# Masked attention on one core: the context division on GpSimd, moments split over VectorE and ScalarE, inverse sums from repeated columns

## The reference

```
q = heads(x @ Wq + bq);  k = heads(x @ Wk + bk);  v = heads(x @ Wv + bv)
scores = einsum('bhqd,bhkd->bhqk', q, k) / sqrt(64)
probs  = softmax(scores + where(adj, 0, -9e15), axis=-1)
ctx    = einsum('bhqk,bhkd->bhqd', probs, v)
y      = x + ctx @ Wf + bf
out    = (y - mean(y)) / sqrt(var(y) + 1e-5)
```

## Time and profile before

| what | value |
|---|---|
| time of three runs | median 1284.17 us (1280.67 to 1289.34) |
| the profiled execution: its time | 1280.71 us |
| the profiled execution: its span | 1278.9 us |
| busy PE / DVE / ACT / POOL | 1177.3 / 1057.7 / 737.2 / 655.1 us |
| DMA moved, mean rate | 251.66 MB, 197 GB/s |
| mean granted clock of TensorE | 0.986 |

### The profile page before, as it was taken

One profiled execution on the slowest core, in us unless ns is written; L12 is line 12 of the kernel. 1 busy time (PEld: TensorE's weight loads), 2 busy tenths in 40 slices (PEclk: granted clock), 3 DMA queues, 4 the chain that ended last, 5 costly groups with the idle time before them and its releaser, 6 DMA issues.

```text
span 1278.9 us, 23768 instructions
## 1 busy us (share of the span) xinstructions
PE 1177.3 (92%) x8406; PEld 867.3 (68%) x8406; DVE 1057.7 (83%) x1619; ACT 737.2 (58%) x1404; POOL 655.1 (51%) x956
## 2 busy tenths in 40 slices
PE   6998999999999899989999899998999999998874
PEld 5866777666776677666776667766677666776642
DVE  5788887988789887889869889698887988789882
ACT  4665665656556575566655565555664656555540
POOL 1335662646536565474545665355762656535533
PEclk9999999999999999999999999999999999999997
DMA  5678877897778877888877978779877897868883
GB/s 163 148 192 234 190 198 192 201 237 175 201 191 215 228 189 195 198 222 201 205 186 188 237 186 211 181 188 248 190 195 186 205 242 176 206 165 204 211 195 96
DMA packets 111607, 251.66 MB, mean 197 GB/s; under 512 B 27904, under 2 KB 62336, under 8 KB 111488
## 3 DMA queue, kind: packets, MB, share of 16 engines
q1 hardware_dynamic: 111488, 250.13, 78.9%
HBM read 36.11 MB, written 12.58 MB: 38 GB/s over the span
## 4 chain that ended last, share of the span: by engine, by line
PE 53%; SPq 16%; DVE 16%; ACT 5%; issue 4%; DMA 3%; POOL 2%; DVEq 0%; POOLq 0%
PE context_ps L515 17%; SPq L307 15%; PE score_ps L500 13%; PE job_ps L406 7%; DVE prob L683 7%; PE job_ps L408 6%; PE job_ps L407 6%; ACT prob L606 5%; DVE prob L676 5%; DMA prob_t<-prob 3%; PE job_ps L437 2%; DVE res L700 1%; DVE stats L707 1%; POOL xt_lo L793 1%; SPq L370 1%
## 5 line engine op out<-in xcount | busy, mean ns | idle before, releaser
L606 ACT ACTIVATE prob<-prob,row_min 128x1024 f32<-128x1024 f32 x384 | 440.9, 1149 | 252.8 <-DVE row_min L676 252.8
L676 DVE CUSTOM_DVE_ANT_0 prob<-score_ps,mask 128x1024 f32<-128x1024 f32 x384 | 454.7, 1221 | 144.8 <-PE score_ps L500 122.7
L683 DVE STREAM_TRANSPOSE prob<-prob 128x1024 f32<-128x1024 f32 x384 | 458.9, 1233 | 31.7 <-ACT prob L606 31.7
L515 PE MATMUL context_ps<-prob_t,v_all 128*64 128x256 f32 x3072 | 359.8, 388 | 40.0 <-DMA prob_t<-prob 39.8
L515 PEld LDWEIGHTS context_ps<-prob_t,v_all 128*64 128x64 f32 x3072 | 236.0, 140 | 151.3 <-issue 58.6
L775 POOL TENSOR_SCALAR mask<-adj_in 128x1024 f32<-128x1024 uint8 x64 | 68.1, 1064 | 169.6 <-DVE row_min L676 156.2
L500 PE MATMUL score_ps<-k_hi,q_hi 64*128 64x512 f32 x768 | 140.7, 444 | 10.5 <-DVE row_min L676 9.7
L809 POOL TENSOR_TENSOR context_lo<-context,context_hi 128x256 fp32r<-128x256 f32 x96 | 70.6, 735 | 142.0 <-ACT context_hi L613 142.0
L406 PE MATMUL job_ps<-xt_hi,weight_hi 128*128 128x256 f32 (+1 forms) x423 | 142.5, 337 | 0.6
L797 POOL TENSOR_TENSOR q_lo<-raw,q_hi 128x256 fp32r<-128x256 f32 x95 | 69.5, 734 | 139.1 <-ACT raw L598 139.1
L407 PE MATMUL job_ps<-xt_lo,weight_hi 128*128 128x256 f32 (+1 forms) x423 | 135.5, 320 | 0.0
(11 more groups left out here) (73 smaller groups left out, 1693.1 us busy)
## 6 DMA issues: line engine op xcount, KB each, us to landing
prob_t<-prob SPq DMA_DIRECT2D x1536, 128.0 KB, 2.4
res<-in_x_dram SPq DMA_DIRECT2D x32, 384.0 KB, 4.0
out_dram<-res SPq DMA_DIRECT2D x32, 384.0 KB, 3.0
x_in<-in_x_dram SPq DMA_DIRECT2D x30, 384.0 KB, 4.1
adj_in<-in_adj_dram SPq DMA_DIRECT2D x31, 256.0 KB, 2.9
res<-in_x_dram SPq DMA_DIRECT2D x1, 768.0 KB, 7.0
prob_t<-in_L_gnn_Wk_dram SPq DMA_DIRECT2D x1, 576.0 KB, 4.3
prob_t<-in_L_gnn_Wq_dram SPq DMA_DIRECT2D x1, 576.0 KB, 8.4
```

Of the source, the lines that this page charges most:

```text
L515: last = pe.matmul(context_ps[64 * head:64 * head + 64, 0:GQ], v_all[:, kt, col:col + HS], keys, start=(kt == 0), stop=(kt == TT - 1))
L606: nc.scalar.activation(probabilities(t), probabilities(t), ACT.Exp, scale=-1.0, bias=row_min[:, ring:ring + 1], accum_out=row_sum[:, s // ...
L676: nc.vector.tensor_tensor_reduce(probabilities(t), in_quarters(score_ps[:, head, :]), in_quarters(mask[:, s % 2, :]), 1.0, HUGE, ALU.add, ...
L683: nc.vector.transpose(probabilities(t), probabilities(t)).then_inc(squared, 1)
```

## The change

The change has eight parts.

1. `divide` moves from VectorE to GpSimd. Since GpSimd's division reads no PSUM, ScalarE first copies `context_ps` to a new tile `context_raw` (`take_context`, behind the slot's exponentials), and GpSimd multiplies `context_raw` by `context`. The next `mix` waits for the copy instead of the division.
2. `add_residual` becomes one `tensor_tensor_reduce`, which also adds up the row, and one small `tensor_scalar` that makes the negated mean. `moments` goes.
3. ScalarE gets `sum_squares`: a Square of the tile with the negated mean as bias, accumulated, at the start of the slot behind the one of the "p" job.
4. Variance plus epsilon and the first guess (`guess_root`) run on VectorE in slots 0, 8, 12, 18, between the masks and the transposes.
5. `make_diagonal` and the ones go. `spread_inverses` multiplies the inverse sums, one column repeated 64 times by an access pattern of step 0, by the identity: four matmuls of 128 columns in place of two of 256. It waits for the reciprocal.
6. GpSimd's order: the division ahead of low parts in its place of the table, `find_root` behind `context_low` in the same slot instead of at the slot's start. In the last slot VectorE refines the root.
7. Slot 9's order is q, x, p in place of q, p, x.
8. The two x loads of slots 11 and 12 (half 1) are issued by ScalarE behind its last eviction of x in slot 11; the last group's second 8 `move` DMAs are issued by ScalarE at slot 24 of the last batch.

```diff
-    9: [("q", 0, 2, 0), ("p", 0, 0, 0), ("x", 0, 0, 1)],
+    9: [("q", 0, 2, 0), ("x", 0, 0, 1), ("p", 0, 0, 0)],
-X_LOADS = {4: (0, 0), 6: (0, 1), 11: (1, 0), 12: (1, 1)}
+X_LOADS = {4: (0, 0), 6: (0, 1)}
+GUESSES = {0: -2, 8: -1, 12: 0, 18: 1}
...
             def spread_inverses(b, job):
-                pe.wait_ge(diag_done, at(b, GROUPS, job[1] + 3))
-                for head in range(2):
-                    last = pe.matmul(job_bank(b.mode, job)[64 * head:64 * head + 64, 0:GQ], ones[:],
-                                     diag[:, 2 * head:2 * head + 2, :], start=True, stop=True)
+                group = job[1]
+                pe.wait_ge(inverted, at(b, GROUPS, group + 1))
+                for qt in range(2):
+                    for head in range(2):
+                        col = 2 * head + qt
+                        last = pe.matmul(job_bank(b.mode, job)[64 * head:64 * head + 64, qt * P:(qt + 1) * P],
+                                         inv_sum[:, group % 2, col:col + 1].to_broadcast([P, HS]), ident[:],
+                                         start=True, stop=True)
...
             def mix(b, group):
-                pe.wait_ge(context_done, at(b, GROUPS, group + 2))
+                pe.wait_ge(context_out, at(b, GROUPS, group + 2))
...
+            def sum_squares(b, n):
+                group, tile = n // 2, n % 2
+                act.wait_ge(mean_done, at(b, TT, n + 1))
+                ...
+                nc.scalar.activation(squares[:], res[:, n % 4, :], ACT.Square, bias=mean_neg[:, n % 4:n % 4 + 1],
+                                     accum_out=square_sum[:, group % 2, tile:tile + 1]).then_inc(squares_summed, 1)
+            def take_context(b, group):
+                act.wait_ge(mixed, at(b, GROUPS, group + 3))
+                act.wait_ge(context_done, at(b, GROUPS, group + 2))
+                nc.scalar.activation(context_raw[:], context_ps[:, 0:GQ], ACT.Copy).then_inc(context_out, 1)
...
@@ ScalarE @@
             def body(b):
                 for s in slots_of(b.mode):
+                    if s > 0:
+                        for job in slot_work(b.mode, s - 1):
+                            if job[0] == "p":
+                                sum_squares(b, job[1])
+                    elif b.mode != "first":
+                        sum_squares(b, -3)
...
+                    if s == SLOTS:
+                        move(nc.scalar, b, GROUPS - 1, 1)
...
-                        if job[0] not in "pm" and job not in early:
+                        if job[0] == "m":
+                            take_context(b, job[1])
+                        elif job[0] != "p" and job not in early:
                             evict(b, job)
+                            if job == ("x", FT - 1, 0, 1):
+                                for i in range(2):
+                                    load_x(nc.scalar, b, 1, i)
...
@@ VectorE @@
             def add_residual(b, job):
-                nc.vector.tensor_tensor(res[:, n % 4, :], job_bank(b.mode, job)[:, 0:H], res[:, n % 4, :],
-                                        ALU.add).then_inc(sum_done, 1)
-            def moments(b, n):
-                ...
+                nc.vector.tensor_tensor_reduce(res[:, n % 4, :], job_bank(b.mode, job)[:, 0:H], res[:, n % 4, :],
+                                               1.0, 0.0, ALU.add, ALU.add,
+                                               row_total[:, n % 4:n % 4 + 1]).then_inc(sum_done, 1)
+                dve.wait_ge(sum_done, at(b, TT, n + 9))
+                nc.vector.tensor_scalar(mean_neg[:, n % 4:n % 4 + 1], row_total[:, n % 4:n % 4 + 1], -1.0 / H, None,
+                                        ALU.mult).then_inc(mean_done, 1)
+            def guess_root(b, group):
+                dve.wait_ge(squares_summed, at(b, TT, 2 * group + 2))
+                nc.vector.tensor_scalar(var_eps[:, two], square_sum[:, two], 1.0 / H, EPS,
+                                        ALU.mult, ALU.add).then_inc(var_done, 1)
+                ...
...
@@ GpSimd @@
+            def divide(b, group):
+                pool.wait_ge(context_out, at(b, GROUPS, group + 3))
+                pool.wait_ge(job_out, out_through(b, ("i", group, 0, 0)))
+                nc.gpsimd.tensor_tensor(context[:], context_raw[:], context[:], ALU.mult).then_inc(context_done, 1)
...
                     work = slot_work(b.mode, s)
                     for job in work:
+                        if job[0] == "m":
+                            divide(b, job[1])
                         if job[0] in "kqx":
                             low_part(b, job)
...
                     for group in contexts_split(b.mode, s):
                         context_low(b, group)
+                    if s in ROOTS and (ROOTS[s] >= 0 or b.mode != "first"):
+                        find_root(nc.gpsimd, b, ROOTS[s])
```

More of the change, by code:

```diff
@@ L300, in scale_rows @@
                 n = (2 * group + tile) % 4
-                engine.tensor_scalar(res[:, n, :], res[:, n, :], mean_var[:, group % 2, tile, 0:1],
+                engine.tensor_scalar(res[:, n, :], res[:, n, :], mean_neg[:, n:n + 1],
                                      inv_dev[:, group % 2, tile:tile + 1],
-                                     ALU.subtract, ALU.mult).then_inc(normalised, 1)
+                                     ALU.add, ALU.mult).then_inc(normalised, 1)
         def move_square(queue, group, a, c):
@@ L309, in move_square, with load_x, find_root, result @@
                             ).then_inc(landed[group % 2], 16)
+        def load_x(queue, b, half, i):
+            last_x = ("x", FT - 1, 1 - half, 1)
+            if half == 0 and b.mode == "first":
+                queue.wait_ge(job_done, 3)
+            else:
+                queue.wait_ge(job_done, done_through(b, last_x, 1 - half))
+            row = S + (4 * half + 2 * i) * P
+            queue.dma_start(x_in[:, 2 * i:2 * i + 2, :], x_rows[bass.ds(at(b, S, row), GQ), :].rearrange(
+                "(t p) h -> p t h", p=P)).then_inc(x_loaded[i], 16)
+        def find_root(engine, b, group):
+            engine.wait_ge(guess_done, at(b, 4, group + 1))
+            guess, var = inv_dev[:, group % 2], var_eps[:, group % 2]
+            ops = 0
+            def result(instruction):
+                nonlocal ops
+                ops += 1
+                instruction.then_inc(root_ops, 1)
+                engine.wait_ge(root_ops, at(b, 4 * ROOT_OPS, group * ROOT_OPS + ops))
+            for _ in range(NEWTON_STEPS):
+                result(engine.tensor_tensor(newton[:], guess, guess, ALU.mult))
+                result(engine.tensor_tensor(newton[:], newton[:], var, ALU.mult))
+                result(engine.tensor_scalar(newton[:], newton[:], -0.5, 1.5, ALU.mult, ALU.add))
+                result(engine.tensor_tensor(guess, guess, newton[:], ALU.mult))
+        def move(queue, b, group, part):
+            queue.wait_ge(squared, at(b, UNITS, 4 * group + 4))
+            queue.wait_ge(mixed, at(b, GROUPS, group + 1))
+            for ahead in (2 * part, 2 * part + 1):
+                for a in range(4):
+                    move_square(queue, group, a, (a + ahead) % 4)
         block = ctx.enter_context(nc.Block())
@@ L382, in body @@
                         load_residual(b, RES_LOADS[s])
[L383 to L384 removed]
+                    if s % 2 == 1 and (s < SLOTS - 1 or b.mode != "last"):
+                        move(sp, b, s // 2, 1)
                     if s % 6 == 1 and (s // 6 < 3 or b.mode != "last"):
@@ L725, in body @@
                         mask_scores(b, 2 * s + 1)
+                        if s in GUESSES and (GUESSES[s] >= 0 or b.mode != "first"):
+                            guess_root(b, GUESSES[s])
                         turn_squares(b, 2 * s)
                         turn_squares(b, 2 * s + 1)
-                    for job in work:
-                        if job[0] == "m":
-                            divide(b, job[1])
                     if s < SLOTS and s % 2 == 1:
```

112 lines of the change are left out of this document (30 added, 82 removed).

## The result

| | before | changed |
|---|---|---|
| median of 14 runs each, us | 1286.57 | 1291.9 |
| lowest to highest, us | 1280.67 to 1290.63 | 1289.97 to 1296.98 |
| profiled execution: its own time, us | 1280.71 | 1290.07 |
| its span, us | 1278.9 | 1288.3 |
| mean granted clock | 0.986 | 0.974 |

The ratio of the changed kernel to the one before is 1.0048, 95% interval 1.003 to 1.0066: half a per cent slower, where 1.25% faster was forecast. By the bound used in the prediction (1%) that is no change, but its sign is plain. The profiled execution of before was one of its fastest, so the two spans lie 9.4 us apart and the medians 5.3; for the size of an effect the ratios are used, and the traces for its place.

The account below looks back on a forecast made before the run. TensorE, busy 92%, was bounded by a chain of waits through slots 8 to 18. Seven batches gave 12.6 us, the last batch 1.2, the tail 2.2: 16 off 1284.2 gives 1268, range 1259 to 1277.

Parts of the forecast that it names:

- SyncE and DMA: Slots 11 to 14: two x loads moved to ScalarE land group 5's squares earlier, gaining 0 to 0.6 us, 0.4 taken.
- the split of the tail: Last group's 16 DMAs issued from two engines take 8.1 us instead of SyncE's 10: 2 us less.
- The two divisions of slots 10 to 12 and the one of slots 16 to 18: Divisions leaving VectorE shorten the chain: 0.78 us for the two, 0.31 for the one.
- the 0.4 for it: VectorE's small tensor_scalar, bounded by 0.17 and 1.65 us, taken at 0.4 because GpSimd is busy half the time.
- 0.17 to 0.2 throughout: Test on VectorE's new small multiply: 0.2 to 0.6 us expected; at 0.17 to 0.2 throughout, the stall behind GpSimd was imagined.
- The second rival: TensorE pays for the small matmuls: each "i" job 1.02 instead of 0.65 us, 1287 us, no change; 12%.
- The wait of slot 9: TensorE's wait for context_lo, 1.3 us in each batch's slot 9 (12.5 us in nine waits), goes.
- The third rival: ScalarE stands behind GpSimd's late divisions in slots 8-10, 12-14, 18-20, delaying exponentials: 1299 to 1315 us; 13%.
- The first rival: Whole idle of slots 8 to 18 closes and slot 14's half clock stops in most batches: 1252 us; 15%.

Follow-up runs that it names:

- e1: The changed kernel with the two x loads of half 1 issued by SyncE again in slots 11 and 12: 0.9901 of the kernel before.
- e5: e1 with the division back on VectorE, straight from PSUM, and no copy on ScalarE: 0.9878 of the kernel before.
- e8: The kernel before with the new residual and moments alone, including ScalarE's squares, the guess and the root behind context_low: 0.9877.
- e4: The changed kernel with 28 and 22 useless matmuls ahead of mix(4) and mix(6), to keep TensorE from idling: 1.0037 of the kernel before.
- e7: The changed kernel without the two x loads of half 1, 768 KB a batch left out: 0.9836 of the kernel before.
- e2: The kernel before with one edit alone: ScalarE issues both x loads of half 1 behind its last eviction of slot 11: 1.0157.
- e9: The changed kernel with both x loads issued by SyncE behind group 4's 16 squares and ahead of group 5's: 0.9935 of the kernel before.
- e12: The kernel before with GpSimd's scale_rows adding the mean instead of subtracting it, which leaves out centring: 0.9989.
- e10: The changed kernel with one x load left on ScalarE and the other issued by SyncE in slot 12: 1.0016 of the kernel before.

## Why the prediction was wrong, step by step

**The step that failed is the one headed SyncE and DMA.** It took the two loads to ScalarE as "gain between 0 and 0.6, I take 0.4" a batch. Measured, they cost 2.7 us a batch. The step saw only what an x load does to SyncE's sequencer (0.58 us between the halves of group 5) and argued "the bytes are the same". It placed them beside group 5's squares, but at the end of slot 11 they are issued ahead of the last one to four squares of group 4, which then took 4.3 to 6.1 us to land in place of some 2.3 and kept `mix(4)` and the mask of slot 12 waiting. The same bytes in another order of issue make another landing late, even if their sum is the same. Neither end of the bound allowed for a loss, and none of the rivals was a landing made late by the loads. The Trainium skill (DMA: Bandwidth & Descriptors, Issuing engines are not separate DMA queues) says that DMAs of different engines interleave on the same 16 DMA engines, and that issuing from several saves only the sequencer's time. The trace agrees in its DMA view (72.0% and 18.2% side by side); the prediction used the second half of that rule for the tail and overlooked the first half here.

**The sum without that step was about right, in part by luck.** It forecast 16 us in all, of which 2.8 were this step's and 2 the split of the tail, so 11.2 for the rest and 13.2 with the split. e1, which has both, gained 0.99%, 12.7 us. But its terms divide otherwise. Against the kernel before, counted from slot 7 as a mean over batches 1 to 6, e1 is 1.9 us ahead at the start of slot 10, where the sum had 0.7, has 0.9 left at slot 13, and its whole batch is 1.6 us shorter; forecast were 1.8, 0.4 of it for the loads. The split of the tail brought 0.3 us and not 2. The two divisions of slots 10 to 12 and the one of slots 16 to 18, 1.1 us a batch in the sum, brought nothing that e1 and e5 or e8 can tell.

**VectorE.** Groups of the changed kernel (columns as in the earlier trace rows):

```profile
L750 DVE CUSTOM_DVE_ANT_0 res<-job_ps,res 128x384 f32<-128x384 f32 x64 | 33.8, 528 | 20.4 <-PE job_ps L427 20.4
L754 DVE TENSOR_SCALAR mean_neg<-row_total 128x1 f32<-128x1 f32 x64 | 9.9, 154 | 2.2
L763 DVE TENSOR_SCALAR inv_dev<-var_eps 128x2 int32<-128x2 int32 x32 | 9.7, 303 | 1.1
L760 DVE TENSOR_SCALAR var_eps<-square_sum 128x2 f32<-128x2 f32 x32 | 6.6, 205 | 1.6 <-ACT squares L639 1.6
```

A block is 0.528 plus 0.083 for the read-out plus 0.154: 0.77, where 0.85 was taken. The new multiply of one column took 0.153 to 0.156 us in all 64 cases, though 52 of them began while a GpSimd instruction ran, so the 0.4 for it was too much. The operations on two columns do stall: the six of 32 guesses that began while GpSimd prepared a residual took 0.85 to 0.94 us and ended within 0.03 us of the end of its instruction, as in the earlier trace rows. The prediction's own test, "0.17 to 0.2 throughout", says that for the new multiply the stall was imagined. VectorE's busy time of batch 3 fell by 9.3 us (130.34 to 121.05), where 6 to 7 were taken.

**TensorE.** The spread came out as taken, at no change:

```profile
563.48 0.66 PE L459 MATMUL job_ps<-ident,inv_sum 128*64 128x128 f32 x8 [1.10 <-DVE row_total L750]
```

Eight records in 0.66 us against 0.65 for four in the earlier trace rows, and 63.2 us of busy time in all, 63.1 before. Slots 0 to 6 and 19 to 23 kept their length. The second rival didn't occur.

**GpSimd and ScalarE.** The wait of slot 9 went, as forecast: 12.5 to 3.7 us, and slot 9 of batch 3 takes 4.9 us after 6.4. The step gave the credit to the root's place and to the new order of slot 9; e8 keeps the old order and its slot 9 takes 5.2 us, for the reason given above. The third rival's condition was more than 1.1 us of lateness; ScalarE's waits for the division are 78.5 us in 74 times, 1.06 on average and at most 2.1. Its sign was exponentials that start over 1 us behind the mask: in the changed kernel two of 384 do, and the mean is 0.1 us. e1, which has all these waits, loses nothing by them that its interval shows. That rival gave 1299 to 1315 for another reason than the one that came; a time near it proves nothing for it. All squares ran at 0.618 plus 0.189 us (0.70 was taken) and the table was never loaded again.

**The tail.** The split was to bring the last landing 2 us nearer. The chain of the changed kernel there:

```profile
1262.81 0.72 ACTq L308
1263.56 5.09 DMA prob_t<-prob
1268.78 5.25 PE context_ps L538 x32
```

and SyncE's half of the same group:

```profile
1257.10 6.25 SPq L308 DMA_DIRECT2D prob_t<-prob  x8
```

The issues end at 1264.42, 2.7 us sooner behind the last transpose (1257.07) than SyncE's 10 us would have it, but the landing takes 5.09 instead of 2.44. From the last transpose to `mix(11)` it is 11.7 us; 12.0 before, 11.96 in e8, which has no split. So 0.3 us of the 2: the term used 259 GB/s, and 2.10 MB in 11.7 us are 179. The two halves were issued side by side, and each of SyncE's squares took longer to land than the one before it, 2.8 us the first and 5.2 the last. The rest of the tail, from the start of `mix(11)` on, takes 19.5 us in both kernels; the root on VectorE took 2.45 us, 2.4 were taken.

**The half clock.** The first rival priced it at half of 3.5 us a batch. e4 took most of it away for no gain that can be told, but paid for it with matmuls of its own, so its price stays open. Why e1 and e8 stop at 1% while SyncE and the landings still bound slots 12 to 16 was followed only as far as e7: 8 us of it are the bytes of these loads.

## What to carry to other kernels

Before moving a transfer to another engine's queue, find out where it will fall in the order of issue of both queues, and who waits for the landing of what is issued behind it. Here loads 0.3 us behind the last square delayed nothing, and loads 1 us ahead of it made slot 12 some 6 us longer. Bound such a move from those landings, not from the 0.6 us of issue that it saves, and let the bound reach below nothing. A place given by the other engine's program ("at the end of slot 11") isn't a fixed place in the first queue. When a change bundles several edits, a small loss can be a good one and a bad one together; run the cheapest edit alone first.

## What the runs showed of the hardware that was not expected

- Two loads of 384 KB issued from ScalarE's queue ahead of the last one to four of 16 squares of 128 KB in SyncE's queue left the squares issued before them as they were (2.3 to 2.6 us to landing for those issued 0.2 to 1.2 us ahead) and made those issued behind them land in 4.3 to 6.1 us (changed kernel, batches 1 to 6). Issued 0.26 us behind the last square they delayed none of them (batch 0, 2.2 to 2.5 us).
- Moving them so raised the time from the last issue of the squares to the use of their landing from 1.9 to 5.2 us (e2, a mean of six batches); issued behind all 16 in SyncE's own queue they left it at 2.0 (e9).
- 16 squares issued from two queues landed no faster than from one: 11.7 against 12.0 us, though their issue ended 2.7 us sooner.
- GpSimd's tensor_scalar of 128x384 with two scalars by row took 1.650 us with subtract and multiply and 0.662 with add and multiply, nothing else changed (e12).
- VectorE's tensor_scalar on one column took 0.154 us in all 64 cases, 52 of which began while a GpSimd instruction ran; of those on two columns, the ten that began well inside a GpSimd instruction ended within 0.03 us of its end (after 0.22 to 0.94 us). The kernel before shows it for the same GpSimd instructions (the low parts) under which most of the 52 ran free: there 22 of 32 operations of line 714 began while one ran, mostly a low part, and took 0.36 to 0.74 us.
- A single load of 384 KB issued from ScalarE took 0.37 to 0.44 us of its queue (e10), one from SyncE 0.57 to 0.60 with few exceptions; the second of two in a row on ScalarE took 0.50 to 0.76 (changed kernel). With both queues issuing squares in the tail ScalarE's took 0.54 to 1.01, SyncE's 0.51 to 1.02.
